# Cross attention keeps three pairs of score banks; self attention's scores and turned weights move into the bank of the small products

## What is computed

```python
x = x + _L0_xattn_ref(ctx, ctx, _layernorm(x), mask, ...)   # 16 heads of 16, softmax over 4096 keys
x = x + _L0_attn_ref(_layernorm(x), ...)                    # 16 heads, softmax over the top 64 of 256 scores
x = x + _L0_ffn_ref(_layernorm(x), ...)                     # one of 8 experts, capacity 128
x = x + _L1_xattn_ref(_layernorm(x), ctx, ...)              # one head, 4096 keys
...
```

## Time and profile before

| | before |
|---|---|
| median of 3 runs | 1747.94 us (1747.13 to 1749.30) |
| the profiled execution's own time | 1751.04 us |
| its span in the trace | 1749.5 us |
| PE busy, share of the span | 1460.3 us, 83% |
| DVE busy | 1332.3 us, 76% |
| ACT busy | 1001.4 us, 57% |
| POOL busy | 273.2 us, 16% |
| mean granted clock of TensorE | 0.913 |

### The profile page before, as it was taken

The page is one execution under the profiler, slowest core; times in us unless marked ns, Lnnn a source line. Parts: engine busy times, 40 slices in busy tenths (PEclk is TensorE's granted clock), DMA queues, the critical chain, the costliest instruction groups (busy, mean ns, idle before and its releaser), DMA issues.

```text
span 1749.5 us, 30718 instructions
## 1 busy us (share of the span) xinstructions
PE 1460.3 (83%) x11490; PEld 894.0 (51%) x11490; DVE 1332.3 (76%) x3956; ACT 1001.4 (57%) x1603; POOL 273.2 (16%) x246
## 2 busy tenths in 40 slices
PE   4999899998988998998986979679888888876666
PEld 2555556655655555555554557347346535632223
DVE  4111079997778786878888899998897787789994
ACT  2788777776665774666761343266485546626520
POOL 5001012222122212122112222211100100010000
PEclk9999999999898997999996889979899989988887
DMA  9555332332202201202104212114444332323330
GB/s 171 111 134 129 69 74 71 76 86 51 35 16 50 49 14 38 49 1 49 38 2 125 73 48 74 61 37 122 109 134 125 104 108 79 97 60 91 85 78 6
DMA packets 70871, 128.21 MB, mean 73 GB/s; under 512 B 15265, under 2 KB 38697, under 8 KB 67633
## 3 DMA queue, kind: packets, MB, share of 16 engines
q1 hardware_dynamic: 70704, 126.04, 30.0%
HBM read 124.70 MB, written 1.31 MB: 72 GB/s over the span
## 4 chain that ended last, share of the span: by engine, by line
PE 49%; DVE 23%; issue 17%; ACT 8%; POOL 3%; DMA 0%; POOLq 0%; DVEq 0%; SPq 0%; ACTq 0%
PE ps L392 16%; PE ps L404 10%; ACT attn_arena L1229 4%; DVE attn_late L1637 4%; DVE attn_late L1774 3%; PE ps L632 3%; DVE attn_top L1771 3%; PE ps L531 3%; PE ps L512 3%; DVE attn_late L1634 2%; PE ps L682 2%; DVE attn_mx L1580 2%; PE ps L495 2%; PE ps L520 2%; PE ps L723 1%
## 5 line engine op out<-in xcount | busy, mean ns | idle before, releaser
L1229 ACT ACTIVATE attn_arena<-ps 128x1024 f32<-128x1024 f32 x512 | 496.5, 1023 | 250.9 <-PE ps L392 249.6
L1771 DVE MAX8 attn_top<-attn_late 128x8 f32<-128x256 f32 x1024 | 380.8, 413 | 39.8 <-ACT attn_late L1251 39.8
L1774 DVE MATCH_REPLACE8 attn_late<-attn_top,attn_late 128x256 f32<-128x256 f32 x1024 | 411.1, 409 | 0.0
L392 PE MATMUL ps<-attn_arena 32*128 32x256 f32 x4096 | 377.0, 416 | 6.5 <-ACT attn_arena L1229 4.4
L404 PE MATMUL ps<-attn_arena 128*32 128x256 f32 x4096 | 289.8, 401 | 4.5 <-issue 4.1
L392 PEld LDWEIGHTS ps<-attn_arena 32*128 32x128 f32 x4096 | 253.6, 192 | 76.2 <-issue 42.2
L1122 POOL TENSOR_SCALAR attn_late<-attn_late 128x512 f32<-128x512 f32 x64 | 95.6, 1494 | 627.9 <-DVE attn_late L1774 627.9
L404 PEld LDWEIGHTS ps<-attn_arena 128*32 128x32 f32 x4096 | 110.6, 112 | 144.9 <-issue 86.3
L1373 ACT ACTIVATE attn_arena<-attn_early,attn_arena 128x255 f32<-128x255 f32 x256 | 108.8, 497 | 98.1 <-DVE attn_late L1637 90.5
L682 PE MATMUL ps<-attn_late,ident 128*128 128x512 f32 x256 | 141.1, 681 | 17.7 <-DVE attn_late L1639 17.7
L1637 DVE TENSOR_TENSOR_SCAN attn_late<-attn_arena,attn_late 128x1024 f32<-128x1024 f32 x64 | 147.6, 2306 | 6.7 <-ACT attn_arena L1373 4.5
(11 more groups left out here) (224 smaller groups left out, 1737.7 us busy)
## 6 DMA issues: line engine op xcount, KB each, us to landing
attn_arena<-ctxT SPq DMA_DIRECT2D x128, 256.0 KB, 6.3
attn_late<-rows SPq DMA_DIRECT2D x64, 512.0 KB, 5.0
attn_arena<-ctxV SPq DMA_DIRECT2D x16, 1024.0 KB, 13.2
attn_arena<-maskT SPq DMA_DIRECT2D x32, 512.0 KB, 4.4
attn_arena<-ctx SPq DMA_DIRECT2D x32, 512.0 KB, 4.1
attn_arena<-w SPq DMA_DIRECT2D x2, 1024.0 KB
X<-x SPq DMA_DIRECT2D x4, 256.0 KB, 3.1
out<-X SPq DMA_DIRECT2D x4, 256.0 KB, 4.8
```

Of the source, the lines that this page charges most:

```text
L392: mm = pe.matmul(ps[:, first + j - 2 * i, u * S:(u + 1) * S], kx[n % 2][rows, k0:k0 + P], qpad[rows, n % GROUPS, b * S:(b + 1) * S], start ...
L1229: act.activation(probs[m % 2][:, 2 * i:2 * i + 2], ps[:, first:first + 2, :], ACT.Exp, scale=1.0 / 16.0).then_inc(exp_done, 1)
L1771: dve.max(top[:, t, turn], s[:, i, t] if turn == 0 else work[:, i, t]).then_inc(picked, 1)
L1774: dve.match_replace(work[:, i, t], top[:, t, turn], s[:, i, t] if turn == 0 else work[:, i, t], LOW).then_inc(picked, 1)
```

## The change

It has four parts:

- Cross attention's scores rotate through the three pairs of banks in all 512 units.
- Self attention's scores of the heads 0 to 46, and the turned weights of the heads 0 to 44, go into bank 7 as two more uses per step. Later heads have banks 5 and 6 as before. DVE, POOL and SP wait for the matching semaphores.
- PE's order: `scores` (slot 1) and `products` (slot 2) stand between `cross_scores` and `cross_products` of their slot. `turn_acc` and `make_v` move from slot 3 to slot 2, `turn_heads` from slot 0 to slot 1, and for the batches 0 and 1 "out", "logits", "h" and "place" move from slot 3 to slot 2 of the same step. DVE takes these products in turn 6 of the same step instead of turn 1 of the next.
- ACT's order: the copies out of bank 7 that belong to the slot before stand ahead of the exps, `take_scores` (slot 1) and `take_sums` (slot 2) between the two exps, and `soft` behind them.

```diff
-RING_UNITS = 144
+SCORES_APART = 47
+TURNED_APART = 45
 DUE = {
-    "ao": [(19, 1), (35, 1), (49, 1), (65, 2)], "out": [(19, 3), (35, 3), (49, 3), (66, 3)],
-    "xm": [(21, 1), (37, 1), (51, 3), (67, 2)], "logits": [(23, 3), (39, 3), (52, 3), (68, 3)],
-    "h": [(24, 3), (40, 3), (53, 3), (69, 3)], "place": [(27, 3), (43, 3), (55, 3), (70, 3)],
+    "ao": [(19, 1), (35, 1), (49, 1), (65, 2)], "out": [(19, 2), (35, 2), (49, 3), (66, 3)],
+    "xm": [(21, 1), (37, 1), (51, 3), (67, 2)], "logits": [(23, 2), (39, 2), (52, 3), (68, 3)],
+    "h": [(24, 2), (40, 2), (53, 3), (69, 3)], "place": [(27, 2), (43, 2), (55, 3), (70, 3)],
 def unit_bank(unit):
-    return (0, 2, 5)[unit % 3] if unit < RING_UNITS else 2 * (unit % 2)
+    return (0, 2, 5)[unit % 3]
...
-                    if last_user(unit) >= 0:
-                        pe.wait_ge(exp_done, last_user(unit) + 1)
+                    if unit >= 3:
+                        pe.wait_ge(exp_done, unit - 2)
...
-                pe.wait_ge(s_copied, p)
+                if p < SCORES_APART:
+                    begin("scores", p)
+                else:
+                    pe.wait_ge(s_copied, p - SCORES_APART)
+                bank = M_ if p < SCORES_APART else S_
...
             def turn_pm(p):
                 pe.wait_ge(pm_ready, p + 1)
-                pe.wait_ge(pT_ready, p)
+                if p < TURNED_APART:
+                    begin("turned", p)
+                else:
+                    pe.wait_ge(pT_ready, p - TURNED_APART)
+                bank = M_ if p < TURNED_APART else T_
...
                     if m is not None:
                         cross_scores(m)
+                    if slot == 1 and 0 <= p + 1 < B * H and (p + 1) % H:
+                        scores(p + 1)
+                    if slot == 2 and 0 <= done < B * H:
+                        products(done)
+                    if m is not None:
                         if m:
                             cross_products(m - 1)
...
                     if slot == 0:
                         if 0 <= done < B * H:
                             turn_pm(done)
+                    if slot == 1:
+                        if ending and d == 0:
+                            turn_acc(h, GROUPS - 1)
                         if ending and d == 1:
                             turn_heads(h, m if m is not None else CROSS_ITS - 1)
...
                     if slot == 2:
-                        if 0 <= done < B * H:
-                            products(done)
-                        if ending and d == 2:
-                            make_qk(h, 0)
-                    if slot == 3:
                         n = (p - FIRST_P) // CROSS_PER - 1
                         if (p - FIRST_P) % CROSS_PER == 0 and 0 <= n < B * GROUPS and n % GROUPS < GROUPS - 1:
                             turn_acc(n // GROUPS, n % GROUPS)
+                        if ending and d == 2:
+                            make_qk(h, 0)
+                        if 0 <= p < B * H and p % H == 0:
+                            make_v(p // H)
...
+                    b, q = p // H, p % H
+                    if slot == 0:
+                        if 0 <= p < B * H and q in (3, 7, 11):
+                            take_qk(b, (q + 1) // 4)
...
+                    if slot == 1:
+                        if 0 <= done < B * H:
+                            take_pT(done)
...
+                    for b in due_before("ao", p, slot):
+                        take_misc(flat_c(aoT), M_, "ao", b)
...
                     if m is not None:
-                        cross_exp(m)
+                        cross_exp(m, 0)
+                    if slot == 1 and 0 <= p + 1 < B * H and (p + 1) % H:
+                        take_scores(p + 1)
+                    if slot == 2 and 0 <= done < (B - 1) * H - 1:
+                        take_sums(done)
+                    if m is not None:
+                        cross_exp(m, 1)
                         if m % PAIRS_OF_KT == 0 and m:
                             copy_acc(m // PAIRS_OF_KT - 1)
...
+                    if slot == 0 and 0 <= p < B * H:
+                        soft(p)
+                    if slot == 1 and ending and d == 1:
+                        act.wait_ge(misc_taken, misc["bad", h] + 1)
+                        way = act.value_load(general[0:1, h:h + 1])
...
             def between(p, turn):
                 if turn == 1:
-                    n = (p - 1 - FIRST_P) // CROSS_PER - 1
-                    if (p - 1 - FIRST_P) % CROSS_PER == 0 and 0 <= n < B * GROUPS and n % GROUPS < GROUPS - 1:
-                        divide(n // GROUPS, n % GROUPS)
-                    if p - 1 >= 0 and (p - 1) // H < B and (p - 1) % H == 0:
-                        add_v((p - 1) // H)
+                    moe_steps(due_after, p)
...
                 if turn == 6:
+                    n = (p - FIRST_P) // CROSS_PER - 1
+                    if (p - FIRST_P) % CROSS_PER == 0 and 0 <= n < B * GROUPS and n % GROUPS < GROUPS - 1:
+                        divide(n // GROUPS, n % GROUPS)
+                    if 0 <= p < B * H and p % H == 0:
+                        add_v(p // H)
+                    moe_steps(due, p, 2)
```

More of the change, by code:

```diff
@@ L1120, in keep_top @@
                 if p:
-                    pool.wait_ge(pm_turned, p)
+                    if p <= TURNED_APART:
+                        pool.wait_ge(misc_made, misc["turned", p - 1] + 1)
+                    else:
+                        pool.wait_ge(pm_turned, p - TURNED_APART)
                 pool.tensor_scalar(pm[:], work[:, i], LOW, None, ALU.is_equal).then_inc(sel_ready, 1)
@@ L1191, in _ @@
                         pool.sem_inc(ohsum_ready, 1)
-                for b in due_after("place", p):
+                for b in due_after("place", p) + due("place", p, 2):
                     root(roots[0])
@@ L1222, in _, with cross_exp @@
         def _(act):
-            def cross_exp(m):
-                if m >= 2:
+            def cross_exp(m, i):
+                if m >= 2 and i == 0:
                     act.wait_ge(pv_done, m - 1)
-                for i in range(2):
-                    act.wait_ge(scores_made, 2 * m + i + 1)
-                    first = unit_bank(2 * m + i)
-                    act.activation(probs[m % 2][:, 2 * i:2 * i + 2], ps[:, first:first + 2, :], ACT.Exp, scale=1.0 / 16.0).then_inc(exp_done, 1)
+                act.wait_ge(scores_made, 2 * m + i + 1)
+                first = unit_bank(2 * m + i)
+                bank = ps[:, first:first + 2, :]
+                act.activation(probs[m % 2][:, 2 * i:2 * i + 2], bank, ACT.Exp, scale=1.0 / 16.0).then_inc(exp_done, 1)
             def copy_acc(n):
@@ L1414, in _ @@
                         copy_acc(B * GROUPS - 1)
-                    if slot == 0:
-                        if 0 <= p < B * H:
-                            soft(p)
-                        b, q = p // H, p % H
-                        if 0 <= p < B * H and q in (3, 7, 11):
-                            take_qk(b, (q + 1) // 4)
-                        if ending and d == 1:
-                            act.wait_ge(misc_taken, misc["bad", h] + 1)
-                            way = act.value_load(general[0:1, h:h + 1])
-                            with act.If(way > 0):
-                                general_batch(h)
@@ L1439, in _ @@
-                    if slot == 3:
-                        if ending and d == 0:
-                            take_sums(done) if done >= 0 else None
-                            take_misc(general[:, h:h + 1], M_[:, 0:1], "bad", h)
-                        elif ending and d == 2:
-                            take_scores(p + 1)
-                        elif 0 <= done < B * H:
-                            take_sums(done)
-                    taken = lambda name: due_before(name, p, slot)
-                    for b in taken("ao"):
-                        take_misc(flat_c(aoT), M_, "ao", b)
@@ L1458, in _ @@
+                    if slot == 1 and ending and d == 1:
+                        act.wait_ge(misc_taken, misc["bad", h] + 1)
+                        way = act.value_load(general[0:1, h:h + 1])
+                        with act.If(way > 0):
+                            general_batch(h)
+                    if slot == 3 and ending and d == 2:
+                        take_scores(p + 1)
                     if slot == 0:
@@ L1473, in _ @@
                     if slot == 2:
-                        for b in due_after("logits", p):
+                        for b in due_after("logits", p) + due("logits", p - 1, 2):
                             gates(b)
@@ L1674, in ffn_add, with moe_steps @@
                 dve.wait_ge(y_used, unit + 1)
+            def moe_steps(which, *at):
+                for b in which("out", *at):
+                    dve.wait_ge(bo_added, b + 1)
+                    add(b, "out")
+                    normalise(norms[0], X[:, b * T:(b + 1) * T], xm).then_inc(xm_ready, 1)
+                    norms[0] += 1
```

(13 more changed lines are left out.)

111 lines of the change are left out of this document (50 added, 61 removed).

## The result

The changed kernel takes 1815.01 us (median of 4 runs, 1806.01 to 1822.46) against 1748.62 before (median of the four runs made for the comparison, one more than in the table ahead of the prediction): a ratio of 1.0392, 95% interval 1.0355 to 1.0430. That is 45 us above the upper end of my range.

What follows compares the result with a forecast made beforehand. DVE bounds batch 0 only; in the next batches' long stretches PE and DVE wait for each other. Terms -13.5+13+2+0+1 = +2.5 us on the profiled 1751.04, taken as 0: forecast 1748 us, range 1731 to 1770.

Steps and rivals of the forecast that it cites:

- the shared bank: Rival: ACT late at both early hand-offs of bank 7, 1.5 us in some 23 steps, +35, 1783 us; chance 0.07.
- One bank for the chain turned, scores, sums: Bank 7: PE waits 0.6 us per step for ACT's copy of the turned weights, 0 behind a wait for DVE.
- T: T(p) is the time when PE ends the turn in slot 0 of step p.
- -13.5 us, if TensorE keeps its clock: Steps 16 to 28 and 32 to 44: 4.6 and 8.9 us less, before any loss of clock.
- +13 for the clock: Same two long stretches: cost of clock falls behind PE's new slot-0 waits; ends 0 and +23, or twice that.
- 0 each, between -3 and +3: Ends of cross attention, steps 13 to 15, 29 to 31, 45 to 47: no change expected in us.
- +2, between 0 and +5: Batch 0, DVE-bound with PE's part covered: add_v comes 2 us early for PE, the three divides at most 0.5.
- Seven of twelve falling: Estimate that seven of twelve slot-0 waits before binding steps drop the clock, 1.9 us per iteration: +13 us.
- The cold rival: Rival: all twelve slot-0 waits drop PE's clock, half for two iterations, +20, 1768 us; chance 0.20.
- T(p+1) = T(p)+x+d+6.5: Step rule for turn 6: x is when the product is finished behind T, d DVE's work on it; divide 14.3 us.
- The third pair: Cross attention's score banks: PE no longer waits for the exp two units back, saving 0.53 and 0.58 us per step.
- The later steps: Later heads: add_v of step 48 in turn 6, +1 us.

Runs made afterwards that it cites:

- changed_soft_later: The changed kernel with ACT's copy of the turned weights ahead of `soft` in slot 1 instead of behind it: 1761.62 us, ratio to before 1.0125.
- own_banks_turn1: The changed kernel with the banks of before and DVE's products back in slot 3 and turn 1, keeping PE's and ACT's new orders: 1727.11 us, ratio 0.9881.
- shared_two_pairs: shared_turn1_soft_later with two pairs of score banks instead of three from unit 144 on: 1729.98 us, ratio to before 0.9923.
- shared_turn1_soft_later: The changed kernel with DVE's products back in slot 3 and turn 1, and the copy of the turned weights ahead of `soft`: 1694.74 us, ratio 0.9732.
- all_edits: The changed kernel with that copy ahead of `soft`, slot 2's products taken in turn 1, and PE's and ACT's old orders in steps without cross attention: 1673.37 us.

## Why the prediction was wrong

**The step that failed is the one on the shared bank**, "One bank for the chain turned, scores, sums": a wait of 0.6 us where PE is the later one, 0 behind a wait for DVE. PE's idle time there is 1.1 us at the 24 times it shows. In step 21 the copy ended 2.2 us behind T where I had 1.7: ACT ended its exps 0.2 us behind T, and a copy of the accumulator, `soft` and the copy of the turned weights followed. The size was half, but the weight was what I missed: I added 0.6 us to a step and gave "the shared bank" a chance of 0.07. Taking the wait out of the changed kernel takes 53 of the 66 us off, by the ratios 2.7 of the 3.9% (`changed_soft_later`). What is left, 1.25% or 22 us against its own runs of before, is still more than my +2.5, and some 12 of it lie in the steps 48 to 63 (237.5 us against 225.6). Up to step 44 the terms then hold rather well, which shows where the sum broke:

- The two long stretches: "-13.5 us, if TensorE keeps its clock", +13 for the clock. Without the hand-over they take 184.9 and 191.2 us, before 183.9 and 191.8: gain and cost cancel, as forecast. With it they take 196.1 and 204.5.
- The ends of cross attention, "0 each, between -3 and +3": from select 12 to 16 and 28 to 32 they take 79.6 and 82.2 us in the changed kernel, 70.6 and 68.8 before, and 67.2 and 71.8 without the hand-over.
- Batch 0, "+2, between 0 and +5", with PE's part covered: from select 0 to 12 it takes 167.4 us, before 157.2, without the hand-over 159.3. "Covered" was wrong with the hand-over in: the cover was 10.6 us of PE's idle time, and an iteration at 1.2 GHz costs 1.9 us of it, and in step 4 two of them, with the sums between, ran at that level.

**The clock.** "Seven of twelve falling" counted the waits in slot 0 alone, and none behind the hand-over. In the changed kernel 16 and 18% of the clock are missing in the two stretches, so TensorE spent about 69 us (2 x 0.16 x 216.7) and 80 us there at 1.2 GHz, against 20 and 29 before. But of the hand-over's 42 us only 9 came back when PE was kept busy in the wait, and of turn 6's 67 us 16. Each loss by itself is thus order by half or more. Where both stand together the clock weighs more: filling slot 0 gave 36 us, and taking the hand-over out lowered the time at 1.2 GHz from 461 to 372 us by the estimate used above, which can be up to 45 of the 53. The cold rival was right that the clock falls, but put it down to the waits in slot 0 alone.

**The sync at turn 6** was worked out right in its rule: T(p+1) = T(p)+x+d+6.5, and PE waits in the next slot 0. The waits in the profile after are 2.06 us behind a divide (expected 2.3), 5.55 behind "out" (5.9) and 6.68 behind "place" (6.9):

```profile
539.42 1.11 PE L523 MATMUL ps<-ident,attn_late 128*128 128x128 f32 x4 [5.55 <-POOL attn_late L1131]
571.73 0.66 PE L523 MATMUL ps<-ident,attn_late 128*128 128x128 f32 x4 [2.06 <-POOL attn_late L1131]
675.67 1.11 PE L523 MATMUL ps<-ident,attn_late 128*128 128x128 f32 x4 [6.68 <-POOL attn_late L1131]
```

From the end of the divide's product (L407, 565.29) to the end of PE's turn (572.39) it is 7.1 us, the rule's 7.0. But the product was ready 9.9 us behind T where I had 7.2: the hand-over's 1.12 us and a stretch at 1.2 GHz lie in between, so that the step took 17.0 us instead of 14.2. What I didn't ask is what the change would be worth without turn 6. With turn 1 and the copy ahead of `soft` the same banks take 1681 us: turn 6 eats 81 us of `changed_soft_later`, all of what the third pair (35 us) and the new orders (20 us, `own_banks_turn1`) bring and more.

**The third pair**, 1.1 us per step, some 33 us over the 30 steps or so where PE is the later one: 35 us measured (`shared_two_pairs`). **The later steps**, +1: 9 us in the changed kernel's profile, and the old orders bring most of it back; the sum had no term for the new orders there. Of the marks I had set, three came true: scores unpaced, PE's idle time ahead of the turned weights about doubled (48.9 to 91.5 us), a clock below 0.93. DVE's waits at the divides were to be 1 to 3 us; at the nine divides of turn 6 they were 1.1 to 7.1 us, seven of them above 3:

```profile
565.33 0.21 DVE L1541 RECIPROCAL attn_recip<-ps 128x8 f32<-128x8 f32 x1 [7.08 <-PE ps L407]
```

And the mark for the shared bank, above 1 us per step, was set far too high: 0.5 us as a mean over the 47 steps, 1.1 in half of them, was enough.

The Trainium skill's rule in "Perfetto Trace Analysis", section "Optimizing Tensor Performance" (independent matmul groups rotate through different banks), was cited against this half of the change. The runs bear it out both ways: the third pair gains 35 us, and the shared bank loses 42 to 53 us as long as the next group waits for the emptying. They also show its limit: with the emptying ahead of ACT's other work the shared bank costs nothing that can be seen (`shared_turn1_soft_later` has the third pair's 35 us in full over `shared_two_pairs`, which shares the bank too, and that one takes 1729.98 against 1728.27 with own banks).

What stays open: the two losses together are larger than their sum (9 us for the banks with turn 1, 40 with turn 6). The time at 1.2 GHz grew by enough to account for it, and filling slot 0 took as much of it back, but no run shows by which waits it grew; the one timeline read, in step 4, has a fall behind a wait of 1.12 us and none behind one of 1.14.

## What to carry to other kernels

In this kernel two engines do about the same work per step, and they needed slack where they met: the product had to be taken early in the consumer's next step, so that the producer had most of a step before it needed that consumer again. When a bank becomes shared, put its emptying first in the emptying engine's order; a hand-over wait of 1 us in half of the steps or more cost more here than the whole third buffer brought. And ask of every sum that comes out near zero what it would be without its largest cost: here two moves in the order of the work took the kernel from 3.9% slower to 3.8% faster than before.

## What I had not expected of the hardware

- Work that nobody reads can pay: 60 matmuls put into waits of PE took 36 us off the changed kernel (1815.0 to 1779.0) and raised the profiled executions' mean granted clock from 0.866 to 0.895.
- An idle time of 1.12 us at 303 us was followed by 10 us at 1.2 GHz, where I had looked at one of 2.13 us; one of 1.14 us at 278 us was followed by none. The length of a wait alone didn't tell.
- Two changes that added 35 and 61 us at 1.2 GHz by themselves (estimates from the granted clock) added 177 together.
- In `all_edits` the granted clock stayed at 1.00 for two stretches of 155.6 us, although PE was idle for 4 to 6 us in each (busy 150.0 and 152.0).
